# A graph network kernel: step tables of 32-bit words for the adjacency build, and its start moved to the 9th gather group

## The chip, the cores and the metric

The kernel runs on one core of a Trainium2 chip. The metric is the device time of one execution in microseconds (us), lower is better. An execution has four compute engines that run side by side: PE (TensorE, matmuls), DVE (VectorE), ACT (ScalarE) and POOL (GpSimd), and SP (SyncE), which issues transfers. Each has an instruction queue of its own, taken in order. They wait for each other on semaphores.

## The reference, cut to what matters

6,250 nodes of 128 features, 100,000 edges sorted by destination. Four graph layers in series, each added to its input. The third (`L2` in the reference) is itself three mean-aggregating layers over the same edges:

```python
def _sage_layer(x, src, dst, Wl, Wr, bias, n_nodes):
    msg_sum = jax.ops.segment_sum(x[src], dst, num_segments=n_nodes)
    cnt = jax.ops.segment_sum(jnp.ones((src.shape[0], 1), x.dtype), dst, num_segments=n_nodes)
    mean = msg_sum / jnp.maximum(cnt, 1.0)
    return mean @ Wl + x @ Wr + bias
...
h = jnp.maximum(_layernorm(x, axis=-1), 0.0)
x = x + _L0_gnn_ref(h, ...)
...
x = x + _L1_gnn_ref(h, ...)
...
x = x + _L2_gnn_ref(h, edge_index, L2_gnn_W_agg, L2_gnn_W_root, L2_gnn_b)
...
x = x + _L3_gnn_ref(h, ...)
```

## The kernel before, in words

The program walks eight internal layers, `k` = 0 to 7. The edges are cut into 784 tiles of 128, the tiles into 98 groups of 8. In the edge layers POOL gathers the source rows of each tile from DRAM by indirect DMA (L958), eight per group into one of two halves of `rows`. PE multiplies each tile by a one-hot matrix of its destinations (L1452), DVE adds the product into `acc` (L1925) and makes the one-hots two groups ahead (`make_onehot`, L1901). The gathers of a group wait until PE has multiplied the group two before.

Layer `k` = 2 does this and, beside it, **builds a dense adjacency matrix** in DRAM that layers 3 and 4 then multiply by (`dense_pass`) without gathering. The build is a chain of 1,567 steps. A step is one edge tile laid against one window of 8 destination nodes: 784 tiles and 784 windows in order are merged into one sequence. In step `i`:

- DVE (`mask_step`, L2068 and L2069) makes two masks: low digit of the source, and high digit of the source together with the place in the window. It may be up to 8 steps (`RING`) ahead of PE.
- PE (`adjacency_step`, L1430 to L1433) waits for the masks (`masked`) and for the evacuation two steps back (`evacuated`). It opens the next step's bank with a tiny matmul of zeros (L1431, 4 columns), then adds the outer product into this step's bank (L1432, 392 columns, bf16). There are four PSUM banks, 3 to 6.
- ACT (`evacuations`, L1097 to L1099) waits for that step (`stepped`) and for its own last evacuation (`evacuated`), and copies the bank's 49 x 8 words into a slab in `H`. SP writes a finished slab, 1,568 KB, to DRAM (`store_slabs`).

Which bank, which tile and which slab column belong to step `i` depends on the data, so the engines read them from tables in SBUF into registers. These loads stand in the engines' queues: PE loads 32 words of 16 bits every 16 steps (L1427), DVE 16 words of 16 bits every 16 steps (L2064), ACT 16 words of 16 bits and one more every 8 steps (L1108, L1111). The program is unrolled; register arithmetic (`FUSED_REGOPS` in the profile, `ISA` in the order of instructions) turns a register into an address behind the waits of its instruction.

The tables are made at the start of layer 2 (`plan`): DVE compares tile ends with step numbers (`compare_tiles`, L1989), PE sums the comparisons (`count_tiles`, L1412), DVE turns the sums into digits (`plan_steps`, L2008 to L2035). This takes four parts of up to 512 steps, and a fifth for the slabs (`plan_stores`). A part takes two groups, beginning at group `PLAN_FROM` = 2. The steps begin at group `STEP_FROM` = 14, 1,567 steps over 84 groups, which `steps_by` spreads evenly. In a group PE has its eight gather matmuls first and then its 18 or 19 steps. DVE runs `LEAD` = 6 masks ahead, then adds the eight products with masks in between. In groups 1 to 13 PE and DVE also have the dense products of the 13 chunks of nodes (`turn_rows`, `multiply_rows`, `take_product`), one chunk per group.

Of the kernel before, what the change touches and what calls it, by code (L numbers as in the profile page):

```python
# [15 lines left out]
P = 128  # L16
# [11 lines left out]
HT = 8  # L28
# [48 lines left out]
LOAD_REGS = 16  # L77
PLAN_FROM = 2
STEP_FROM = 14
# [9 lines left out]
def build(nc, a, out):  # L89
    ds = bass.ds  # L90
    with ExitStack() as ctx:
# [135 lines left out]
        def turned_at(k, c):  # L227

            at = 2048 if k in SAGE else 2560 + c % 2 * 512
            return PS[:, at:at + width(c)]  # L230

        def product_at(k, c):
            at = 2560 if k in SAGE else c % 2 * 512
            return PS[:, at:at + width(c)]

# [12 lines left out]
        def slack(k):  # L248
            return 0 if k in SAGE else 1
# [187 lines left out]
        counted_ps = PS[:, 6 * 512:7 * 512]  # L437
# [572 lines left out]
        def _(s):  # L1010
# [82 lines left out]
            evac_regs = [s.alloc_register(f"evac{j}") for j in range(2 * WN)]  # L1093

            def evacuate(i, first):
                s.wait_ge(stepped, i)
                s.wait_ge(evacuated, i)  # L1097
                to = H[:, ds(first[WN + i % WN], SLAB_WORDS)].rearrange("p (h d) -> p h d", d=SLABW)[:, :, 0:WN]
                nc.scalar.activation(to, PS[:, ds(first[i % WN], MASKW)].rearrange("p (h d) -> p h d", d=WN), ACT.Copy)\  # L1099
                    .then_inc(evacuated, 1)  # L1100

            def evacuations():
                s.wait_ge(tables_ready, 1)
                s.wait_ge(table_stored, 16 * table_parts[2])
                for i in range(STEPS + 1):
                    if i % WN == 0:
                        at = i // WN * 3 * WN
                        s.load(evac_regs, act_table[:, at:at + 2 * WN])  # L1108
                        first = [s.snap(r, min_val=3 * 512, max_val=6 * 512) for r in evac_regs[0:WN]]
                        first += [s.snap(r, min_val=0, max_val=SLAB_WORDS + SLABW - WN) for r in evac_regs[WN:2 * WN]]  # L1110
                        freed = s.value_load(act_table[:, at + 2 * WN:at + 2 * WN + 1], min_val=16, max_val=16 * SLABS)  # L1111
                        s.wait_ge(slabs_moved, freed)
                    if i > 0:
                        evacuate(i, first)
                    else:
                        s.wait_ge(edges_counted, PLANS + 2)
                        to = H[:, ds(first[WN], SLAB_WORDS)].rearrange("p (h d) -> p h d", d=SLABW)[:, :, 0:WN]
                        nc.scalar.activation(to, PS[:, ds(first[0], MASKW)].rearrange("p (h d) -> p h d", d=WN), ACT.Copy)\
                            .then_inc(evacuated, 1)
# [143 lines left out]
        def _(pe):  # L1263
# [158 lines left out]
            bank_regs = [pe.alloc_register(f"bank{j}") for j in range(2 * LOAD_REGS)]  # L1422
            bank_at = []

            def adjacency_step(i):
                if i % LOAD_REGS == 0:
                    pe.load(bank_regs, pe_table[:, 2 * i:2 * (i + LOAD_REGS)])  # L1427
                    bank_at[:] = [pe.snap(r, min_val=3 * 512, max_val=6 * 512 + MASKW) for r in bank_regs]
                wait(pe, evacuated, i - 1)
                pe.wait_ge(masked, i + 1)  # L1430
                mm(PS[:, ds(bank_at[LOAD_REGS + i % LOAD_REGS], 4)], ones_bf[:], zeros_bf[:, 0:4], start=True, stop=True)  # L1431
                mm(PS[:, ds(bank_at[i % LOAD_REGS], MASKW)], lo_slot(i), mask_slot(i), start=False, stop=True,  # L1432
# [1098 lines left out]
```

## Time and profile before

| | us |
|---|---|
| median of 3 runs | 11355.47 (11355.42 to 11371.14) |
| profiled execution | 11347.99 |
| its span | 11346.2 |

| engine | busy us | share of the span |
|---|---|---|
| PE | 5627.2 | 50% |
| DVE | 5247.5 | 46% |
| POOL | 4841.9 | 43% |
| ACT | 2131.4 | 19% |

The span is the time from the first to the last instruction of the profiled execution; its own device time is 1.8 us longer. No engine is busy for much over half of the span, so a share says little: each stage has its own limit, and has to be read apart. The granted clock of PE is given as a share of 2.4 GHz. Operations on registers and loads into them are not counted as busy; the idle time that they cause is shown as "issue".

### The profile page before, as it was taken

What the parts mean: (1) busy time and instruction counts of PE and PEld (TensorE: products, weight loads), DVE (VectorE), ACT (ScalarE), POOL (GpSimd) and SP (SyncE); (2) the same over time, 40 slices, a digit from 0 to 9 for tenths busy, and PEclk for the clock granted to TensorE, in tenths of its full rate; (3) what the DMA queues carried; (4) which work ended last, traced back from release to release, by engine and by line L of the source; (5) the groups of instructions that cost most, each with busy time, mean ns of one, the idle gap of its engine ahead of it and who ended that gap; (6) DMA issues with size and microseconds to landing.
All of it is one profiled execution on the core that took longest, in us unless ns stands there. A gap on an engine that the chain in (4) does not pass through costs nothing. (4 is left out here: it accounts for less than half of the span.)

```text
span 11346.2 us, 113568 instructions
## 1 busy us (share of the span) xinstructions
PE 5627.2 (50%) x27414; PEld 3519.3 (31%) x27414; DVE 5247.5 (46%) x17197; ACT 2131.4 (19%) x3703; POOL 4841.9 (43%) x5045
## 2 busy tenths in 40 slices
PE   5555555554444444445999804552306442216542
PEld 3333333323222222223444402352203442203432
DVE  6765566656333333443000105873308763219754
ACT  5555433331333333333000000000000000000000
POOL 5666466655222222221000173266570466650664
PEclk7766666666555555556999955566555665555756
DMA  5444456551222222223888721131230321220321
GB/s 163 136 133 140 141 162 172 162 146 49 81 80 81 81 74 81 85 82 111 297 284 291 238 79 36 52 98 41 56 95 6 93 72 36 75 72 19 101 59 34
DMA packets 728976, 1217.62 MB, mean 107 GB/s; under 512 B 109340, under 2 KB 547085, under 8 KB 714832
## 3 DMA queue, kind: packets, MB, share of 16 engines
q1 hardware_dynamic: 552716, 847.76, 22.2%
q0 software_dynamic: 161120, 311.32, 10.6%
q10 hardware_dynamic: 14688, 53.48, 1.2%
q8 instruction: 165, 2.70, 0.1%
q14 instruction: 287, 2.35, 0.1%
HBM read 865.31 MB, written 346.85 MB: 107 GB/s over the span
## 5 line engine op out<-in xcount | busy, mean ns | idle before, releaser
L988 POOL DMA_INDIRECT RO<-table,src_t x2346 | 2256.6, 962 | 3367.4 <-DMA table<-H 1287.9
L958 POOL DMA_INDIRECT RO<-table,src_t x2346 | 2242.8, 956 | 2919.5 <-PE PS L1452 1676.6
L1925 DVE TENSOR_TENSOR acc<-acc,PS 128x128 f32 x3910 | 1098.0, 281 | 1674.0 <-remote 1074.8
L1530 PE MATMUL PS<-RO 128*128 128x128 f32 x3060 | 649.1, 398 | 1136.7 <-DMA RO<-table,src_t 776.2
L1099 ACT ACTIVATE H<-PS x1567 | 779.4, 497 | 1716.3 <-issue 977.6
L1603 PE MATMUL PS<-als_bf,RO 128*128 128x49 bf16 x7056 | 397.4, 218 | 1192.5 <-issue 903.2
L1530 PEld LDWEIGHTS PS<-RO 128*128 128x128 f32 x3060 | 602.3, 301 | 1182.8 <-DMA RO<-table,src_t 797.3
L2363 DVE SCALAR_TENSOR_TENSOR H<-iota_row,srchi_t,PS 128x49 f32<-128x49 f32 x2352 | 461.1, 263 | 1086.2 <-remote 738.6
L1431 PE MATMUL PS<-work,ones_bf 3*128 3x4 bf16 x1567 | 279.3, 178 | 1356.4 <-issue 985.7
L2169 DVE TENSOR_SCALAR RO<-PS,loc_t,shared 128x128 f32<-128x128 f32 x2346 | 943.4, 404 | 0.6
L2068 DVE TENSOR_SCALAR bn<-work,shared 128x128 bf16<-128x128 int16 x1567 | 411.2, 262 | 1123.0 <-PE PS L1432 792.4
L1603 PEld LDWEIGHTS PS<-als_bf,RO 128*128 128x128 bf16 x7056 | 327.5, 118 | 1481.6 <-issue 1144.2
L1431 PEld LDWEIGHTS PS<-work,ones_bf 3*128 3x128 bf16 x1567 | 152.2, 97 | 1885.8 <-issue 1881.9
L1452 PE MATMUL PS<-RO 128*128 128x128 f32 x3128 | 593.5, 366 | 182.7 <-DMA RO<-table,src_t 97.2
L1452 PEld LDWEIGHTS PS<-RO 128*128 128x128 f32 x3128 | 579.9, 279 | 288.1 <-DMA RO<-table,src_t 132.0
L1530 PE MATMUL PS<-RO,H 128*128 128x128 f32 x1632 | 326.3, 382 | 264.6 <-issue 127.4
L1258 ACT ACTIVATE small<-small 128x49 f32<-128x49 f32 x3 | 0.7, 245 | 2283.9 <-issue 2283.9
L2351 DVE TENSOR_SCALAR RO<-PS,iota_col 128x1024 bf16<-128x1024 f32 x294 | 376.7, 1282 | 81.8 <-remote 52.4
L1490 PE MATMUL PS<-GT,H 128*128 128x512 f32 (+1 forms) x966 | 394.1, 565 | 1.4 <-DMA GT<-adjacency 1.4
L1530 PEld LDWEIGHTS PS<-RO,H 128*128 128x128 f32 x1632 | 304.6, 288 | 286.9 <-issue 286.9
L1490 PE MATMUL PS<-GT,acc 128*128 128x512 f32 (+1 forms) x952 | 392.3, 569 | 0.0
L1438 PE MATMUL PS<-shared,mats 128*128 128x512 f32 x392 | 323.4, 952 | 116.6 <-DVE shared L2121 67.7
(398 smaller groups left out, 8827.1 us busy)
## 6 DMA issues: line engine op xcount, KB each, us to landing
GT<-adjacency SPq DMA_DIRECT2D x126, 1792.0 KB, 7.2
adjacency<-H SPq DMA_DIRECT2D x98, 1568.0 KB
RO<-adjacency SPq DMA_DIRECT2D x42, 1792.0 KB, 7.2
RO<-table,src_t POOLq DMA_INDIRECT x4692
staged<-RO ACTq DMA_DIRECT2D x102, 512.0 KB
H<-staged SPq DMA_DIRECT2D x102, 512.0 KB
soft_rows<-shared SPq DMA_DIRECT2D x196, 256.0 KB
H<-soft_rows SPq DMA_DIRECT2D x98, 512.0 KB
```

The costliest lines, as they stand in the source:

```text
L958: pool.indirect_dma_start(rows[:, h * HT + j, :], None, table[k % 2], at(src_t[:, t:t + 1]))\
L988: pool.indirect_dma_start(rows[:, g % 2 * HT + j, :], None, table[k % 2], at(src_t[:, t:t + 1]))\
L1099: nc.scalar.activation(to, PS[:, ds(first[i % WN], MASKW)].rearrange("p (h d) -> p h d", d=WN), ACT.Copy)\
L1431: mm(PS[:, ds(bank_at[LOAD_REGS + i % LOAD_REGS], 4)], ones_bf[:], zeros_bf[:, 0:4], start=True, stop=True)
L1452: last = mm(window_at(k, c, j), rows[:, r, :], onehot[:, r, :], start=True, stop=True)
L1490: last = mm(sums_at(c).rearrange("p (s d) -> p s d", d=SLABW), of[:, t, :], slot_of(n)[:, 0:nslabs(c), j, :], start=(t == 0), stop=(t == N ...
L1530: last = mm(PS[:, o:o + D], block[:, j * D:(j + 1) * D], onehot[:, h * HT + j, :], start=True, stop=True)
L1603: last = mm(PS[:, o:o + NT], hot_bf[:, h, j, :], als_bf[:, part * NT:(part + 1) * NT], start=(part == 0), stop=(part == 2))
L1925: tt(at, at, window_at(k, c, j), ALU.add).then_inc(added[h], 1 if j < n - 1 else HT - n + 1)
L2068: ts(lo_slot(i), iota_16[:, 0:D], slo_t[:, ds(t, 1)], None, ALU.is_equal)
L2169: return ts(onehot[:, c % 2 * HT + j, :], iota_ps, loc_t[:, t:t + 1], ex_t[:, t:t + 1], ALU.is_equal, ALU.mult)
L2363: last = stt(mask[:, j, :], iota_row[:, 0:NT], srchi_t[:, ds(e, 1)], cand[:, j, :], ALU.is_equal, ALU.mult, accum_out=als_t[:, ds(e, 1)])
```

## The change

- `LOAD_REGS` falls from 16 to 8, and the tables are three rows of 32-bit words (`bank_row`, `column_row`, `tile_row`) and a small 16-bit one (`freed_row`), instead of 16-bit tables in which each engine's words stood together.
- PE loads 8 words every 8 steps. Both bank addresses are worked out in registers from one word. ACT loads 8 words every 8 steps and works its bank's address out from the slab column, by a division and a remainder. DVE loads 8 words every 8 steps.
- `plan_steps` has 14 operations instead of 20.
- A part of the plan takes one group instead of two, and DVE turns a part's sums into digits one group after they are counted. `STEP_FROM` is 8: 1,567 steps over 90 groups.
- The dense products take two chunks per group in layer 2, in banks 3 to 6. The plan's sums go to bank 7, which held a copy of `iota`; so the one-hots of layer 2 read `iota_row` in SBUF, and the copy in PSUM is made again in `plan_stores`.

```diff
@@
-LOAD_REGS = 16
+LOAD_REGS = 8
+BANKS = 4
+FIRST_BANK = 3
 PLAN_FROM = 2
-STEP_FROM = 14
+STEP_FROM = 8
@@ def turned_at(k, c) / product_at(k, c)
+            if k == 2:
+                at = 1536 + c % 2 * 512
...
+            if k == 2:
+                at = 2560 + c % 2 * 512
...
+        def chunks_beside(c):
+            return range(max(0, 2 * c), min(NCH, 2 * c + 2))
@@
-        pe_table = G[0:1, 1568:2 * 1568].bitcast(U16)
-        act_table = G[0:1, 2 * 1568:2 * 1568 + 2352].bitcast(U16)
-        dve_table = G[0:1, 2 * 1568 + 2352:2 * 1568 + 2352 + 784].bitcast(U16)
+        bank_row, column_row, tile_row = (G[0:1, (1 + i) * (STEPS + 1):(2 + i) * (STEPS + 1)].bitcast(I32)
+                                          for i in range(3))
+        freed_row = small[0:1, 4 * NT:6 * NT].bitcast(U16)
...
-        counted_ps = PS[:, 6 * 512:7 * 512]
+        counted_ps = PS[:, 7 * 512:8 * 512]
@@ def evacuations()
                 for i in range(STEPS + 1):
-                    if i % WN == 0:
...
-                        s.load(evac_regs, act_table[:, at:at + 2 * WN])
...
+                    if i % LOAD_REGS == 0:
+                        s.load(column_regs, column_row[:, i:i + LOAD_REGS])
+                        to = [s.snap(r, min_val=0, max_val=SLAB_WORDS + SLABW - WN) for r in column_regs]
+                        freed = s.value_load(freed_row[:, i // WN:i // WN + 1], min_val=16, max_val=16 * SLABS)
                         s.wait_ge(slabs_moved, freed)
...
+                    column = to[i % LOAD_REGS]
+                    bank_of = s.snap((column // WN) % BANKS * 512 + FIRST_BANK * 512, min_val=FIRST_BANK * 512,
+                                     max_val=(FIRST_BANK + BANKS - 1) * 512)
+                    wait(s, stepped, i)
+                    wait(s, evacuated, i)
@@ def adjacency_step(i)
                 if i % LOAD_REGS == 0:
-                    pe.load(bank_regs, pe_table[:, 2 * i:2 * (i + LOAD_REGS)])
...
+                    pe.load(bank_regs, bank_row[:, i:i + LOAD_REGS])
...
+                bank_now = bank_at[i % LOAD_REGS]
+                to = pe.snap(bank_now * 512 + FIRST_BANK * 512, min_val=FIRST_BANK * 512,
+                             max_val=(FIRST_BANK + BANKS - 1) * 512)
+                opened = pe.snap((bank_now + 1) % BANKS * 512 + FIRST_BANK * 512 + MASKW,
+                                 min_val=FIRST_BANK * 512 + MASKW, max_val=(FIRST_BANK + BANKS - 1) * 512 + MASKW)
@@ def edge_pass(k), PE
                     if k == 2:
-                        if c % 2 == 1 and 0 <= (c - PLAN_FROM) // 2 <= PLANS:
-                            count_tiles((c - PLAN_FROM) // 2)
+                        if 0 <= c - PLAN_FROM <= PLANS:
+                            count_tiles(c - PLAN_FROM)
@@ def make_onehot(k, c)
+                iota = iota_row[:] if k == 2 else iota_ps
@@ def plan(c), DVE
-                p, rest = divmod(c - PLAN_FROM, 2)
+                p = c - PLAN_FROM
+                if 0 < p <= PLANS:
+                    plan_steps(p - 1)
                 if 0 <= p <= PLANS:
-                    if rest == 0:
-                        compare_tiles(p)
...
+                    compare_tiles(p)
+                if p == PLANS + 1:
+                    plan_stores()
@@ def mask_step(i)
                 if i % LOAD_REGS == 0:
-                    v.load(tile_regs, dve_table[:, i:i + LOAD_REGS])
+                    v.load(tile_regs, tile_row[:, i:i + LOAD_REGS])
```

How the instructions stand before and after, at three places. `ISA` rows are register arithmetic, and `[waits ...]` names the semaphores that a row waits for.

PE in the build, around a register load; before:

```order
L1432 ISA
L1432 MATMUL PS<-cut_row,bn 128x392
L1427 TENSOR_LOAD GT
L1428 ISA x4
L1431 ISA [waits masked,evacuated]
L1431 MATMUL PS<-work,ones_bf 128x4
L1432 ISA
L1432 MATMUL PS<-shared,bn 128x392
```

and after:

```order
L1442 ISA
L1442 MATMUL PS<-cut_row,bn 128x392
L1432 TENSOR_LOAD GT
L1433 ISA
L1441 ISA [waits masked,evacuated]
L1441 MATMUL PS<-work,ones_bf 128x4
L1442 ISA
L1442 MATMUL PS<-shared,bn 128x392
```

The load stands in the same place, 8 words instead of 32, and comes every 8 steps. The `ISA` ahead of the small matmul holds two operations on registers before and six after (an addition, a remainder by 4, two multiplications, two additions); the one ahead of the large matmul two before and four after.

ACT in the build, around a register load; before:

```order
L1099 ACTIVATE H<-PS 128x49x8
L1108 TENSOR_LOAD GT
L1109 ISA
L1110 ISA
L1111 TENSOR_LOAD GT
L1111 ISA x2
L1099 ISA [waits evacuated,stepped,slabs_moved]
L1099 ACTIVATE H<-PS 128x49x8
```

and after:

```order
L1122 ACTIVATE H<-PS 128x49x8
L1113 TENSOR_LOAD GT
L1114 ISA
L1115 TENSOR_LOAD small
L1115 ISA x2
L1122 ISA [waits evacuated,stepped,slabs_moved]
L1122 ISA
L1122 ACTIVATE H<-PS 128x49x8
```

Two `ISA` now stand between the waits and the copy: six operations (a division by 8, a remainder by 4, two multiplications, two additions) and two, where one `ISA` of four stood.

PE ahead of the build, between the gather matmuls of two groups; before:

```order
L1452 MATMUL PS<-RO 128x128 [waits added1]
L1452 MATMUL PS<-RO 128x128 x3
L1318 MATMUL PS<-mats,mid 128x128 [waits p_done,p_copied]
L1318 MATMUL PS<-mats,mid 128x128 x3
L1305 MATMUL PS<-ident,H 128x128 [waits p_copied,h_chunks]
L1305 MATMUL PS<-ident,H 128x128 x3
L1452 MATMUL PS<-RO 128x128 [waits added1,onehot_ready1,gathered1]
```

and after:

```order
L1323 MATMUL PS<-mats,mid 128x128 [waits p_done,p_copied]
L1323 MATMUL PS<-mats,mid 128x128 x3
L1323 MATMUL PS<-mats,mid 128x128 [waits p_done,p_copied]
L1323 MATMUL PS<-mats,mid 128x128 x3
L1310 MATMUL PS<-ident,H 128x128 [waits p_copied,h_chunks]
L1310 MATMUL PS<-ident,H 128x128 x3
L1310 MATMUL PS<-ident,H 128x128 [waits p_copied,h_chunks]
L1310 MATMUL PS<-ident,H 128x128 x3
L1417 MATMUL PS<-cut_row,small 128x512 [waits tiles_compared]
L1417 MATMUL PS<-cut_row,small 128x512 x3
L1417 MATMUL PS<-bn,small 128x512 x3
L1462 MATMUL PS<-RO 128x128 [waits added0,onehot_ready0,gathered0]
```

Each of these groups now has two chunks of dense products, and a count that waits for DVE's comparisons of the same group (`tiles_compared`), ahead of the next group's gather matmuls.

## Rows read from the trace of the kernel before

**Rows 1.** windows of the layer-2 pass: lead-in, build. Columns as in the first line.
```profile
core 0: us, PE busy (x) PEld busy (x) DVE busy (x) ACT busy (x) POOL busy (x), PEclk, DMA share, GB/s
2647.40:2831.00 183.60, 86.15 (x424) 73.94 (x424) 114.87 (x297) 7.45 (x13) 123.70 (x128) 0.65 0.17 46
2831.00:5330.00 2499.00, 1142.88 (x4458) 583.80 (x4458) 1000.61 (x3874) 779.91 (x1569) 620.77 (x654) 0.56 0.22 80
```

**Rows 2.** waits in the build (2831 to 5330 us): us in total, times, longest.
```profile
PE PS L1431 <- issue: 985.7, 127, 11.3
ACT H L1099 <- issue: 977.6, 392, 7.5
```

**Rows 3.** register loads, each from the view of its line: duration ns min/median/max.
```profile
L1427 PEldq TENSOR_LOAD <-GT x98: 7516/10073/10575, 2822.4 to 5305.9; - x98
...
L1108 ACTq TENSOR_LOAD <-GT x196: 3367/3392/6607, 2809.0 to 5319.4; - x196
...
L2064 DVEq TENSOR_LOAD <-GT x98: 3582/3594/4121, 2817.9 to 5297.1; - x98
...
L1057 ACTq TENSOR_LOAD <-rank_row x65: 289/310/917, 1190.2 to 11292.4; - x65
...
L1910 DVEq TENSOR_LOAD <-seg_row x490: 593/597/1756, 61.4 to 11266.2; - x164
```

**Rows 4.** timeline of ACT in the build: start, length, in brackets idle before.
```profile
3519.38 0.50 ACT L1099 ACTIVATE H<-PS  x1 [4.03 <-issue]
3520.07 0.50 ACT L1099 ACTIVATE H<-PS  x1 [0.19 <-ACT H L1099]
...
3526.56 0.50 ACT L1099 ACTIVATE H<-PS  x1 [2.58 <-PE PS L1432]
```

**Rows 5.** timeline of PE in the same stretch.
```profile
3522.61 3.44 PE L1452 MATMUL PS<-RO 128*128 128x128 f32 x16
...
3535.15 0.18 PE L1431 MATMUL PS<-work,ones_bf 3*128 3x4 bf16 x1 [8.35 <-ACT H L1099]
```

**Rows 6.** ACT's register arithmetic and one-register load, by line: ns min/median/max.
```profile
L1099 ACTq FUSED_REGOPS  x1567: 6/55/508, 2834.2 to 5329.2; - x196
...
L1110 ACTq FUSED_REGOPS  x196: 126/126/131, 2812.6 to 5323.6; - x196
...
L1111 ACTq TENSOR_LOAD <-GT x196: 263/269/273, 2812.8 to 5323.8; - x196
L1111 ACTq FUSED_REGOPS  x196: 167/168/191, 2813.1 to 5324.1; - x196
```

**Rows 7.** timeline of DVE in the same stretch.
```profile
3514.10 1.22 DVE L1901 TENSOR_TENSOR RO<-PS,loc_t 128x1024 f32<-128x1024 f32 x1
...
3519.27 0.25 DVE L2068 TENSOR_SCALAR bn<-work,shared 128x128 bf16<-128x128 int16 x1 [3.05 <-issue]
...
3519.73 0.25 DVE L2068 TENSOR_SCALAR bn<-work,shared 128x128 bf16<-128x128 int16 x1
...
3526.18 0.29 DVE L1925 TENSOR_TENSOR acc<-acc,PS 128x128 f32 x1 [4.16 <-PE PS L1452]
```

**Rows 8.** timeline of DVE ahead of the build.
```profile
2703.81 3.22 DVE L1925 TENSOR_TENSOR acc<-acc,PS 128x128 f32 x8 [6.12 <-remote]
...
2708.68 0.68 DVE L2009 SCALAR_TENSOR_TENSOR GT<-work,PS 128x512 f32<-128x512 int16 x1
...
2718.65 0.43 DVE L2035 TENSOR_SCALAR GT<-GT 128x512 f32<-128x512 f32 x1
...
2725.03 1.13 DVE L1989 TENSOR_SCALAR cut_row<-work,small 112x512 bf16<-112x512 int16 x4
```

**Rows 9.** timeline of PE: a count of the plan, and the build's first step.
```profile
2727.95 1.91 PE L1412 MATMUL PS<-cut_row,small 112*128 112x512 bf16 x4
2729.65 1.20 PE L1412 MATMUL PS<-bn,small 112*128 112x512 bf16 x3
...
2831.11 0.18 PE L1431 MATMUL PS<-work,ones_bf 3*128 3x4 bf16 x1 [4.75 <-issue]
```

More of the change, by code:

```diff
@@ L1091, in normalize @@
                     normalized_rows(k, c - 1)
[L1093 to L1100, printed above, removed]
+            column_regs = [s.alloc_register(f"column{j}") for j in range(LOAD_REGS)]
             def evacuations():
@@ L1420, in open_banks @@
                     .then_inc(edges_counted, 1)
-            bank_regs = [pe.alloc_register(f"bank{j}") for j in range(2 * LOAD_REGS)]
+            bank_regs = [pe.alloc_register(f"bank{j}") for j in range(LOAD_REGS)]
             bank_at = []
@@ L1453, in edge_pass @@
                     last.then_inc(multiplied[h], 1)
-                    if 1 <= c <= NCH:
+                    if k == 2:
+                        for m in chunks_beside(c - 1):
+                            multiply_rows(k, m)
+                        for m in chunks_beside(c):
+                            turn_rows(k, m)
+                    elif 1 <= c <= NCH:
                         multiply_rows(k, c - 1)
-                    if c < NCH:
+                    if k == 0 and c < NCH:
                         turn_rows(k, c)
@@ L2006, in plan_steps @@
                 n = plan_width(p)
+                part = slice(p * PW, p * PW + n)
                 v.wait_ge(edges_counted, p + 1)
-                w = window_cols[:, p * PW:p * PW + n]
+                w = window_cols[:, part]
                 step(stt(w, iota_16[:, 0:n], float(p * PW), counted_ps[:, 0:n], ALU.add, ALU.subtract))
-                step(copy(dve_table[:, p * PW:p * PW + n], counted_ps[0:1, 0:n]))
+                step(copy(tile_row[:, part], counted_ps[0:1, 0:n]))
                 row, a, b = w[0:1, :], int_a[0:1, 0:n], int_b[0:1, 0:n]
-                in_loads = b.rearrange("o (g w) -> o g w", w=LOAD_REGS)
@@ L2013, in plan_steps @@
-                in_eights = b.rearrange("o (g w) -> o g w", w=WN)
-                def digits_of(shift, mask):
-                    step(ts(a, row, float(shift), None, ALU.add))
-                    step(ts(b, a, mask, None, ALU.bitwise_and))
-                digits_of(0, 3)
-                step(ts(by_load(pe_table, p, 0), in_loads, 512.0, 3.0 * 512, ALU.mult, ALU.add))
-                digits_of(1, 3)
-                step(ts(by_load(pe_table, p, 1), in_loads, 512.0, 3.0 * 512 + MASKW, ALU.mult, ALU.add))
@@ L2023, in plan_steps @@
-                digits_of(3, 3)
-                step(ts(by_evacuations(p, 0), in_eights, 512.0, 3.0 * 512, ALU.mult, ALU.add))
-                digits_of(15, 15)
+                step(copy(a, row))
+                step(ts(bank_row[:, part], a, BANKS - 1, None, ALU.bitwise_and))
+                step(ts(a, row, 15.0, None, ALU.add))
+                step(ts(b, a, 15, None, ALU.bitwise_and))
                 step(ts(a, b, 3, None, ALU.arith_shift_right))
                 step(ts(a, a, float(SLAB_WORDS - SLABW), None, ALU.mult))
-                step(stt(by_evacuations(p, 1), in_eights, float(WN), a.rearrange("o (g w) -> o g w", w=WN),
-                         ALU.mult, ALU.add))
+                step(stt(column_row[:, part], b, float(WN), a, ALU.mult, ALU.add))
@@ L2092, in gather_and_build @@
                     if c + 2 < NG:
-                        make_onehot(c + 2)
-                    if 1 <= c <= NCH:
-                        take_product(2, c - 1)
+                        make_onehot(2, c + 2)
+                    for m in chunks_beside(c - 1):
+                        take_product(2, m)
                     plan(c)
@@ L2481, in _ @@
                     step(memset(acc[:], 0.0), zeros_ready)
-                if k == 2:
-                    step(copy(iota_ps, iota_row[:]))
                 if k in DENSE:
```

55 lines of the change are left out of this document (20 added, 35 removed).

## The prediction, made before the changed kernel ran

> **What bounds the kernel now.** I read the windows first. Layer 2 starts gathering at 2647, the build's first step on PE is at 2831.1 and the build ends at 5330: 2,499 us, 22% of the span, in which PE is busy 1,143 us, DVE 1,001, ACT 780, POOL 621 and the DMA engines 22% [rows 1, 9]. No engine is full, so something that is not counted as busy sets the pace. The waits name it: PE and ACT each stood 980 us at "issue", waiting for nothing but their own queue, and PE's 127 such waits reach 11.3 us [rows 2].
>
> The views of the single lines show what the queues did. PE's load of 32 words takes 10.07 us and comes 98 times: 98 x 10.07 = 987 us. ACT's load of 16 words takes 3.39 us and comes 196 times, DVE's of 16 words 3.59 us [rows 3]. The two timelines show the effect. Ordinarily one evacuation follows the other by 0.50 + 0.19 = 0.69 us (3519.38 to 3520.07). At a load of ACT the gap is 4.03 us, at a load of PE 8.35 us; and while PE does the 16 passes of a group's gather matmuls, 3.44 us, ACT drains the two steps in hand and then stands 2.58 us [rows 4, 5]. As a check I add these for the whole build: 987 for PE's loads; 98 x 3.84 = 376 for those of ACT's loads that don't fall beside one of PE's (4.03 - 0.19 = 3.84); 1,568 evacuations x 0.685 = 1,074; 84 groups x 2.4 = 202. That is 2,639, 6% over the 2,499 measured, since some loads begin under gather matmuls. So the model is good to some 6%, on the high side.
>
> **The loads.** The three loads of the build read 16-bit words, at 0.315 us a word on PE, 0.21 to 0.22 on ACT and DVE. But the kernel also has loads of 32-bit words: ACT's of four takes 0.310 us and DVE's of eight 0.597 us, both 0.075 to 0.078 us a word [rows 3]. The changed kernel makes exactly DVE's form, eight 32-bit words, on three engines. I take 0.60 us for each; for PE, whose 16-bit words cost 1.4 times DVE's, 0.84. The upper end for a word is the 16-bit price: 1.7 us on ACT and 2.5 on PE for eight. A lower end is four words' 0.31.
>
> The Trainium skill ("Runtime: NRT & Kernel Launch", Instruction fetch mechanics) states that a TENSOR_LOAD costs about 200 ns a register, even in bulk. By that, eight words would be 1.6 us. The trace agrees for 16-bit words (212 ns) and speaks against it for 32-bit ones (75 ns).
>
> **ACT's step.** The new register arithmetic stands behind both waits of an evacuation, so it lengthens every step of the chain. Before, one `ISA` of four operations takes 0.055 us [rows 6]. After come one of six, with a division and a remainder that the trace shows nowhere, and one of two. Bounds: six plain operations of another kind take 0.126 us (L1110), 0.021 each; three comparisons take 0.168, 0.056 each [rows 6]. At the cheap rate the eight cost some 0.17 us, at the dear one 0.45. I take plain operations at 0.014 (0.055 / 4) and the two unknown ones at the dear 0.056, plus 0.03 to start a second `ISA`: 6 x 0.014 + 0.112 + 0.03 = 0.22, 0.165 more than now. A step becomes 0.685 + 0.165 = **0.85 us**; bounds 0.77 and 1.08.
>
> **ACT's load boundary.** Now 3.84 us over an ordinary gap. It loses 3.39 - 0.60 = 2.79, and L1110 with its start and two operations, 0.19; the one-word load (0.26) and its checks (0.17) stay. 0.86 is left; 0.9 with something for loads of two engines at once, which slow each other (L1108 reaches 6.6 us) [rows 3, 6].
>
> **PE's load boundary.** 0.84 plus one `ISA` of eight, about 0.17: 1.0 us every 8 steps. It runs beside ACT's boundary of 0.9 at the same steps. PE may be two evacuations ahead: from an evacuation's end to the evacuation three further on there are three ACT steps, 2.55 us, and the work in between is some 0.4 us of register work and signals, 0.1 and 0.5 of matmuls and 0.7 on ACT, 1.7 us. The 0.85 us of slack covers the load but for 0.2, which ACT's own boundary covers. So 0; without that cover, 196 x 1.0.
>
> **DVE.** A pair of masks takes 0.46 us (3519.27 to 3519.73), a one-hot of eight tiles 1.2; each group DVE waits 4.2 us for PE's gather matmuls [rows 7]. A group has 17.4 steps: 17.4 x 0.46 = 8.0, eight adds at 0.2 in between 1.6, one-hot 1.2, loads of tiles 2.2 x 0.7 = 1.5, load of segments 1.0, together 13.3, and 17.5 with the wait. That is under the 18.9 us of a group found below, so it is hidden by 1.4 us a group, no more. The one-hot from SBUF instead of PSUM moves as many elements and is taken at the same 1.2.
>
> **Gather matmuls.** Now 2.4 us of ACT's time a group. Two slower evacuations cover 0.33 more; PE's new register work in the restart and mixed clocks leave 2.1 us, in 90 groups. POOL's indirect DMAs, busy 621 us in the build before [rows 1], take 684 for 90 groups, 40% of the new build. A slab comes every 17 us or so; DMA engines at 22% go to about 33%. Neither counts.
>
> **The lead-in.** Up to group 3's adds (2703.8) it is as before. DVE turned a part into digits in 2708.68 to 2719.08, 10.4 us for 20 operations; 14 take about 7.2. Four comparisons take 1.1 us, so seven 2.0 [rows 8]. Groups 3 to 5 each have adds 3.2, one-hot 1.1, two products 1.3, digits 7, comparisons 2 = 14.7. Then PE's count of this group (three of seven matmuls 1.2 us, so about 3 [rows 9]) and the next gather's 3 to 4 come in series, because the count waits for the comparisons: 22 us. Groups 6 and 7 are smaller (a part of 32 steps, then slabs), 15 and 11. 2704 + 3 + 66 + 15 + 11 = 2799, with the first load 2800, against 2831 [rows 9]: **-31 us**, give or take 15.
>
> **The sum.** Build: 1,568 x 0.85 = 1,333, plus 196 x 0.9 = 176, plus 90 x 2.1 = 189: **1,698 us**, against 2,499. Gain 801 + 31 = 832. A group is 1,698 / 90 = 18.9. The profiled execution took 11,348; less 832 is **10,516 us**. It lies 7 us under the median, less than I can resolve. With the bounds of ACT's step alone: 0.77 gives 10,391, 1.08 gives 10,877.
>
> **Rivals.**
> - *DVE takes over.* If the new register operations are as cheap as the old ones (step 0.77), ACT's chain gives 1,573 us and DVE's 17.5 us x 90 = 1,575. Then the time stops at 1,575: 10,393. For it: additions and multiplications cost 14 ns; against: a division is no addition. 0.13.
> - *PE's clock rises.* It was 0.56 in the build, so mostly 1.2 GHz [rows 1], with PE busy 46%; in the new build the same work fills 70%. At 2.4 GHz the gather matmuls halve, and most of 90 x 1.7 = 153 us goes: 10,365. 0.07.
> - *Loads cost by the register, whatever the type.* ACT's eight words at 0.212 are 1.7 us, 1.1 more than taken, x 196 = 216; PE's 2.5 run beside them, but exceed ACT's boundary by half a microsecond: up to 98 more. 10,730 to 10,830. Against it stand two rows of 32-bit loads [rows 3]; for it, that neither is on PE. 0.07. The 200 ns a register of the Trainium skill ("Runtime: NRT & Kernel Launch", Instruction fetch mechanics) would come to the same.
> - *Register division and remainder are dear, though not ruinous*: 0.15 us each instead of 0.056 add 0.19 x 1,568 = 295: 10,810. 0.09.
> - *They cost more than the loads did* (slower). Both stand behind ACT's waits in each of 1,568 steps, and nothing hides them. The gain of 832 is gone at 832 / 1,568 = 0.53 us a step more than taken, so from 0.32 us for each of the two. At 0.4 each the step is 1.54 and the time 10,516 + 0.69 x 1,568 = 11,600. Against it: no register operation in the rows is over 0.056 us. 0.04, of which 0.01 falls within 0.2% of no change.
>
> **How the numbers follow.** My forecast, 10,430 to 10,620, has 0.60. The range must reach DVE's and the clock's case below and part of the dearer ones above: 10,350 to 10,760. Outside lie some 0.05 below and 0.13 above. A difference of 0.2% is about what a measurement of this kernel tells from none. Faster by more than that: every case but the last, 0.96; within it 0.01; slower 0.03.
>
> **What the profile after will show.** Right: TENSOR_LOAD of eight at 0.6 us on ACT and DVE and under 0.9 on PE; register arithmetic of ACT near 0.22 in its two `ISA`; evacuations 0.85 apart, with gaps of 1.2 us every eight; "issue" waits on PE nearly gone; first step at 2800, last near 4500. Wrong: an eight-word load over 1.5 us; ACT's step over 1 us; DVE with no wait for the gather matmuls, or PE waiting for masks in most steps, which makes DVE the bound; a granted clock far over 0.56 in the build; or time that moves into layers 3 and 4.

## The result, and the profile after

The changed kernel takes 10,660.19 us (median of 4 runs, 10,642.40 to 10,671.95) against 11,359.05 us of the kernel before (4 runs, 11,355.42 to 11,371.14): a ratio of 0.9384, 95% interval 0.9373 to 0.9396. The profiled execution took 10,670.19 us, its span is 10,668.4. The forecast was 10,516 with a range of 10,350 to 10,760: the time lies inside, but above the inner 10,430 to 10,620 that I gave 0.60, and of a forecast gain of 832 us only 699 came. Identical programs ran in two kinds of execution here, in which the kernel before takes 11,348 to 11,413 us or 9,600 to 9,612 us; I call them long and short, all of the runs named so far are long ones, and each experiment is read against runs of its own kind.

The windows of the changed kernel, lead-in and build, answer to [rows 1]; the columns are the same.

```profile
core 0: us, PE busy (x) PEld busy (x) DVE busy (x) ACT busy (x) POOL busy (x), PEclk, DMA share, GB/s
2647.40:2803.00 155.60, 60.87 (x334) 51.84 (x334) 92.16 (x252) 15.21 (x37) 77.74 (x78) 0.65 0.15 40
2803.00:4645.60 1842.60, 1182.35 (x4552) 609.83 (x4551) 1042.60 (x3935) 779.33 (x1568) 708.23 (x704) 0.59 0.31 111
```

The build is 1,843 us instead of 2,499, with the same 780 us of evacuations in it. PE's share rises from 46% to 64%, the granted clock only from 0.56 to 0.59: still mostly the lower of its two levels.

The views of the single lines, in order PE's, ACT's and DVE's load, ACT's word on the freed slab, and the register arithmetic of PE's two matmuls and of ACT's evacuation (ns min/median/max), answer to [rows 3, 6]:

```profile
L1432 PEldq TENSOR_LOAD <-GT x196: 587/591/1432, 2800.6 to 4637.1; - x196
...
L1113 ACTq TENSOR_LOAD <-GT x196: 4/547/1711, 2801.2 to 4638.0; - x196
...
L2060 DVEq TENSOR_LOAD <-GT x196: 5/597/2045, 2800.5 to 4630.7; - x196
...
L1115 ACTq TENSOR_LOAD <-small x196: 5/267/885, 2802.0 to 4638.7; - x196
L1115 ACTq FUSED_REGOPS  x196: 14/168/710, 2802.3 to 4639.0; - x196
...
L1441 PEldq FUSED_REGOPS  x1567: 104/104/131, 2802.1 to 4643.5; - x196
...
L1442 PEldq FUSED_REGOPS  x1567: 60/60/70, 2802.3 to 4643.7; - x196
...
L1122 ACTq FUSED_REGOPS  x3136: 4/37/716, 2802.5 to 4645.4; - x196
```

Eight 32-bit words take 0.55 to 0.60 us on all three engines, so PE's loads fell from 987 us in the build to 196 x 0.59 = 116. The last row mixes two instructions of each evacuation, one of six operations at 0.143 or 0.147 us and one of two at 0.037 (when taken apart). Its longest is 0.716 us, where ACT's arithmetic before had a longest of 0.508 [rows 6]. That is the mark of what I had not foreseen.

The waits in the build answer to [rows 2] (us in total, times, longest):

```profile
ACT H L1122 <- PE PS L1442: 625.2, 755, 3.6
ACT H L1122 <- issue: 269.4, 326, 18.9
...
PE PS L1441 <- ACT H L1122: 349.8, 727, 2.9
PE PS L1441 <- issue: 166.1, 256, 3.2
PE PS L1441 <- DVE cut_row L2065: 89.4, 97, 2.2
PE PS L1441 <- DVE shared L2065: 51.7, 90, 2.2
...
DVE acc L1941 <- PE PS L1462: 401.9, 89, 5.3
DVE bn L2064 <- PE PS L1442: 286.8, 423, 2.9
...
POOL RO L970 <- PE PS L1462: 896.6, 87, 15.7
```

PE's "issue" waits have gone from 986 us to 166. Now ACT and PE wait for one another: the ring of steps is the bound. DVE still waits for PE, as it would not if it set the pace.

The timeline of ACT shows an ordinary stretch and then the unforeseen one (columns as in [rows 4]):

```profile
3614.15 0.50 ACT L1122 ACTIVATE H<-PS  x1 [0.34 <-ACT H L1122]
3614.98 0.50 ACT L1122 ACTIVATE H<-PS  x1 [0.34 <-issue]
3615.82 0.50 ACT L1122 ACTIVATE H<-PS  x1 [0.34 <-ACT H L1122]
3616.66 0.50 ACT L1122 ACTIVATE H<-PS  x1 [0.34 <-issue]
3618.92 0.50 ACT L1122 ACTIVATE H<-PS  x1 [1.77 <-issue]
3620.54 0.50 ACT L1122 ACTIVATE H<-PS  x1 [1.12 <-issue]
3621.83 0.50 ACT L1122 ACTIVATE H<-PS  x1 [0.80 <-ACT H L1122]
3622.67 0.50 ACT L1122 ACTIVATE H<-PS  x1 [0.34 <-PE PS L1442]
```

Evacuations start 0.84 us apart. From 3616.66 to 3621.83 three take 5.17 us. One load of ACT's falls in it, so 3.35 would be ordinary; PE does no gather matmul. What stands between them are ACT's short queue instructions (a wait on a semaphore, a register operation): some take 0.70 us here instead of 0.02 to 0.15, and others begin only 0.7 us after the one before. I counted those that take 0.5 us or more in the trace, loads left out: 270 on ACT in the build, 150 on DVE, none on PE, in some 90 stretches of about 4 us, one to each gather group, 6 to 12 us after the start of its first gather on POOL. In the kernel before they were 5 on ACT, 51 on DVE and 4 on PE.

I then took the distance of every two evacuations, and what it exceeds 0.837 us by, or 1.67 at a load. The build of 1,843 us is

| part of the build | us | forecast |
|---|---|---|
| 1,568 steps x 0.837 | 1,312 | 1,333 |
| 196 load boundaries x 0.83 | 163 | 176 |
| excess while PE does a group's gather matmuls, 89 groups x 1.59 | 141 | 189 |
| excess where ACT's short instructions take 0.7 us | 207 | none |
| the rest | 19 | none |

### The profile page after: what moved, and what is told of

It is laid out like the page before. It is cut to its first block and busy times, and to the rows that moved or that the text cites. A ratio compares the mean times of both kernels' runs of the same rounds, so it can differ in the third digit from the quotient of the medians.

```text
span 10668.4 us, 114911 instructions
## 1 busy us (share of the span) xinstructions
PE 5650.2 (53%) x27414; PEld 3518.0 (33%) x27414; DVE 5257.7 (49%) x17169; ACT 2130.5 (20%) x3703; POOL 4883.4 (46%) x5045
## 5 line engine op out<-in xcount | busy, mean ns | idle before, releaser
L1618 PE MATMUL PS<-als_bf,RO 128*128 128x49 bf16 x7056 | 396.9, 218 | 1182.7 <-issue 857.4
L1618 PEld LDWEIGHTS PS<-als_bf,RO 128*128 128x128 bf16 x7056 | 327.4, 118 | 1472.2 <-issue 1075.9
```

Source lines behind the costliest of these rows:

```text
L1618: last = mm(PS[:, o:o + NT], hot_bf[:, h, j, :], als_bf[:, part * NT:(part + 1) * NT], start=(part == 0), stop=(part == 2))
```

## The experiments

**First four runs: which part gives what, and what makes the slow stretches.** The kernel before took 11,413.27 us beside them, a long execution, 54 us over the first. The changed kernel itself did not run beside these four, and each was run once, so differences below some 100 us in them are weak.

*e1_words16*: the tables hold 16-bit words again, still eight to a load (and the plan has one more copy on DVE, not shown).

```diff
-        bank_row, column_row, tile_row = (G[0:1, (1 + i) * (STEPS + 1):(2 + i) * (STEPS + 1)].bitcast(I32)
+        bank_row, column_row, tile_row = (G[0:1, (1 + i) * (STEPS + 1):(1 + i) * (STEPS + 1) + (STEPS + 1) // 2].bitcast(U16)
```

> The changed kernel with its three tables as 16-bit words again, still eight to a load every eight steps. Theory (a word's type sets the price): ACT's load of eight goes from 0.55 to about 1.7 us, PE's from 0.59 to about 2.4, DVE's to 1.8; ACT's load boundary grows by some 1.15 us, so the build by 196 x 1.15 = 225 us, and the time goes to about 10,890. Rival (what costs is more than eight registers in one load, or a load as such): the loads stay near 0.6 us and the time near 10,665.

Measured: 10,892.86 us, build 2,046 us. The loads of ACT, PE and DVE in this kernel:

```profile
L1113 ACTq TENSOR_LOAD <-GT x196: 8/1728/4729, 2803.4 to 4843.5; - x196
...
L1432 PEldq TENSOR_LOAD <-GT x196: 1923/1927/3884, 2802.9 to 4842.7; - x196
...
L2061 DVEq TENSOR_LOAD <-GT x196: 13/1832/4932, 2802.9 to 4835.2; - x196
```

Eight words of 16 bits cost 1.73, 1.93 and 1.83 us, the same eight as 32-bit words 0.55, 0.59 and 0.60. Of the loads only the type differs, so the type sets the price: 0.22 to 0.24 us a word against 0.07. The build grew by 203 us; 196 x (1.73 - 0.55) = 231. Taken apart as above, the load boundaries cost 230 us more, but the stretches of slow short instructions only 120 us instead of 207, and other gaps 58 more. So the time agrees with the expected 10,890 in part by luck; the loads' price does not rest on it. PE's share of the 16-bit price was less than the 0.315 us a word of [rows 3]: with eight words instead of 32 it was 0.24.

*e2_start14*: one line, `STEP_FROM = 14` instead of 8.

> The changed kernel with the steps beginning at group 14 again; all else as changed. Theory (the earlier start is a small part): first step near 2,860 instead of 2,803, six groups fewer beside the build, so the build some 35 us shorter, time about 10,685 (+20). Rival (the earlier start carries the gain): the time goes back by hundreds of us.

Measured: 10,814.32 us, first step 2,882.1 (79 us later), build 1,893 us, 50 longer than the changed kernel's. That is far over the expected 10,685, by more than the 54 us of the kernel before beside it. I had not expected a longer build; the last experiment repeats this kernel.

*e3_few_rows*: the gathers beside the build fetch 8 rows of 128. What the left-out 120 rows would give is missing from layer 2's sums.

```diff
+                        n = 8 if k == 2 and g >= STEP_FROM else P
-                        pool.indirect_dma_start(rows[:, h * HT + j, :], None, table[k % 2], at(src_t[:, t:t + 1]))\
+                        pool.indirect_dma_start(rows[0:n, h * HT + j, :], None, table[k % 2], at(src_t[0:n, t:t + 1]))\
```

> Gathers beside the build fetch 8 of their 128 rows (so layer 2's sums and all after are other numbers); as many instructions and signals as before. In the trace of the changed kernel ACT's queue has one stretch a group, 6 to 12 us after the group's gathers began, in which short instructions take 0.7 us each; 2.3 us of delay a group. Theory G (the gathers' transfers cause it): the stretches vanish, the build falls from 1,842 to about 1,640 us and the time to about 10,460. Rivals (instruction supply, slab stores, VectorE's one-hot): they stay and the time is 10,650 +- 25.

Measured: 10,808.84 us, build 1,959 us, and 274 slow short instructions on ACT, 207 on DVE: no fewer than with all rows. The volume of the gathers does not make the stretches. The time is over both of my cases; by the count above the stretches cost some 315 us here.

*e4_onehot_psum*: DVE reads the row of numbers for its one-hots from PSUM during the build, as before.

```diff
-                iota = iota_row[:] if k == 2 else iota_ps
+                iota = iota_row[:] if k == 2 and c < STEP_FROM + 2 else iota_ps
```

> In the build the one-hots read iota from PSUM again instead of SBUF. Theory P (two SBUF operands of VectorE beside POOL's work cause the slow stretches in the queues): they vanish, time about 10,460. Rival (they come from elsewhere): no change, 10,650 +- 25, one-hot 1.22 us in both.

Measured: 10,781.17 us, build 1,917 us, 297 and 179 slow short instructions, some 275 us of stretches. The reading place does not make them either, and again the time is over both cases. In the changed kernel a one-hot took 1.218 us from SBUF and 1.217 from PSUM, as forecast.

**Next four: the terms of the step, and the changed kernel once more.** Here the kernel before took 9,608.24 us (7 runs, 9,600.16 to 9,612.34): short executions, though on the chip of the first four.

*e5_changed_again*: no edit.

> The changed kernel unaltered, on the chip of the next three: 10,660 on its first chip, 10,670 to 10,730 here if the chip adds what the last one added to before (54 us). Adjacency build 1,843 us, 0.837 us from one evacuation to the next, one slow stretch of ACT's and DVE's queues to each gather group (270 short instructions of 0.7 us on ACT, 150 on DVE).

Measured: 8,717.94 us, ratio 0.9074 (0.9058 to 0.9089), nowhere near the 10,670 to 10,730 expected. So the change gains 890 us here, and 699 in the long executions. The build is 1,643 us, with no slow short instruction on DVE and no slow register operation on ACT.

```profile
core 0: us, PE busy (x) PEld busy (x) DVE busy (x) ACT busy (x) POOL busy (x), PEclk, DMA share, GB/s
2386.80:4030.20 1643.40, 1192.67 (x4553) 616.01 (x4552) 1026.59 (x3936) 779.35 (x1567) 714.62 (x705) 0.60 0.35 124
```

PE, ACT, DVE and POOL are busy for the same time as in the long execution within 2%, and the clock is the same. The 199 us between the two builds are idle time, against the 207 us counted for the slow stretches. By the same count the gather matmuls cost 152 us here, 1.7 a group.

*e6_ahead_of_waits*: ACT forms the bank address into a register ahead of the two waits of a step, and in a shorter form, without the division.

```diff
-                    bank_of = s.snap((column // WN) % BANKS * 512 + FIRST_BANK * 512, min_val=FIRST_BANK * 512,
-                                     max_val=(FIRST_BANK + BANKS - 1) * 512)
+                    s.reg_mod(bank_reg, column, WN * BANKS)
+                    s.reg_mul(bank_reg, bank_reg, 512 // WN)
+                    s.reg_add(bank_reg, bank_reg, FIRST_BANK * 512)
+                    hold(s)
+                    bank_of = s.snap(bank_reg, min_val=0, max_val=8 * 512 - MASKW)
```

> ACT's bank address is formed into a register ahead of the two waits of a step (modulo, product and sum, 0.15 us), instead of behind them. Theory A (an evacuation's period is ACT's and PE's round trip, and the 0.147 us of arithmetic behind the wait lies on it): 0.837 becomes 0.69 to 0.71 us, the build 1,843 less 1568 x 0.14 = 1,620, the time 10,440 to 10,480. Rival B (PE's own step, or the evacuation itself, sets the period): 0.80 or more stays, the build 1,790 or more. If the slow stretches come from the number of instructions that ACT takes in, this kernel, which has one or more further queue instructions per step, shows more than 270 slow ones on ACT; if they go with the gather group's start, the number stays about 90 stretches.

Measured: 8,562.80 us, ratio 0.8914 (0.8899 to 0.8929), 155 us under e5. The instruction behind the waits is short again,

```profile
L1126 ACTq FUSED_REGOPS  x1567: 60/60/65, 2385.2 to 3869.6; - x196
```

and the step is 0.689 us, the 0.15 less that theory A says. Rival B falls. What stands behind the waits went from 0.184 us in two instructions to 0.060 in one. The new form is also cheaper, 0.077 us ahead of the waits (a remainder 0.040, product and sum 0.037) where it had 0.147 behind them; I estimate from these durations that some 0.05 of the 0.15 is the shorter form's and the rest the move's. No run separates the two. Of 1,568 x 0.15 = 235 us the build gave 158 (1,485 us): the gather matmuls now cost some 190 us instead of 152, which I put down to ACT's draining sooner what PE has in store; the distance at a load stayed, 1.70 us where it was 1.67, which costs 34; and 7 went to other gaps.

*e7_split_gather*: four steps between the two halves of a group's gather matmuls.

```diff
+                        if j == 4:
+                            for i in range(steps_by(c - 1), steps_by(c - 1) + split):
+                                adjacency_step(i)
...
-                        for i in range(steps_by(c - 1), steps_by(c)):
+                        for i in range(steps_by(c - 1) + split, steps_by(c)):
```

> A group's eight gather matmuls are given in two halves with four adjacency steps between them, so that PE is away from the steps for about 1.7 us at a time instead of 3.4. Theory A (each group's gather matmuls cost the chain of steps 1.57 us because they are longer than the one step that the ring of four banks holds in store): the excess at gathers falls from 141 to under 60 us, the build to 1,760, the time to 80 less than the changed kernel. Rival: every return of PE costs its own start, two halves cost as much as one whole, and the time stays within 20.

Measured: 8,614.67 us, ratio 0.8965 (0.8950 to 0.8980), 103 us under e5; build 1,537 us, 106 less, and the excess at gathers 47 us instead of 152. The stall at the gather matmuls is what PE's absence exceeds the store by; two short absences cost little.

*e8_all_three*: both edits, with masks 10 steps ahead (`LEAD = 10`) and the word on the freed slab read at the middle of eight steps.

```diff
+                        if i == 0:
+                            freed = s.value_load(freed_row[:, 0:1], min_val=16, max_val=16 * SLABS)
                         s.wait_ge(slabs_moved, freed)
+                    if i % LOAD_REGS == LOAD_REGS // 2 and i + LOAD_REGS // 2 < STEPS + 1:
+                        n = i // WN + 1
+                        freed = s.value_load(freed_row[:, n:n + 1], min_val=16, max_val=16 * SLABS)
```

> Both edits, the word on the freed slab read at the middle of eight steps instead of between the load and the first evacuation, and masks 10 steps ahead of PE instead of 6. If nothing else takes over: 1568 x 0.70 + 196 x 0.55 + 91 x (0.6 + 2.3) = 1,470 us of build. DVE's groups need 17.5 us each, 91 x 17.5 = 1,590, so DVE is likely to take over: build 1,590 to 1,640, time 10,410 to 10,470, 200 to 250 under the changed kernel on this chip.

Measured: 8,452.85 us, ratio 0.8797 (0.8782 to 0.8812): 265 us under the changed kernel and 1,155 under the one before, in short executions. The edits of e6 and e7 alone gave 155 and 103, 258 together, so the further masks and the moved word show no clear gain of their own; the word costs at its new place too (the distance there is 1.48 us in the median, where 0.689 is ordinary).

```profile
core 0: us, PE busy (x) PEld busy (x) DVE busy (x) ACT busy (x) POOL busy (x), PEclk, DMA share, GB/s
2405.90:3781.20 1375.30, 1142.08 (x4551) 601.20 (x4551) 1004.22 (x3935) 778.80 (x1568) 736.78 (x704) 0.62 0.41 148
```

The build is 1,375 us. My 1,590, at which DVE was to take over, was wrong: of the 17.5 us a group that I gave DVE, 4.2 were its wait for PE's gather matmuls, which shrinks when they are split (154 us over 87 waits here, 1.8 each). A group now takes 1,375 / 90 = 15.3 us, PE is busy 83% of it.

**Next three: both kernels in one kind of execution.** Short again (before: 9,604.38 us), on another chip.

*e9_before_again* and *e10_changed_again*: no edits, for a trace of each.

> The kernel before, unaltered, for its trace. The last job's executions of before and of the changed kernel were 1,750 and 1,940 us shorter than the first ones of the same programs, and the changed kernel's build (1,643 instead of 1,843 us) held no slow stretch of ACT's and DVE's queues. If such an undisturbed execution is met again (about 9,608 us): first step at 2,410 to 2,440 us, build 2,440 to 2,500 us, no slow short instruction on DVE where the first trace had 51, and so before's build hardly shorter than the 2,499 us of the first trace. If the disturbance costs both kernels the same in the build, as a mere slowing of everything would, before's build comes out 200 us shorter, at 2,300.

> The changed kernel unaltered beside the last one, once more for its trace. Undisturbed: 8,718 us, build 1,643 us, no slow stretch. Disturbed: 10,660 to 10,730 us, build 1,843 to 1,900 us, 270 slow short instructions on ACT and 150 on DVE. Whichever it is, the run of before beside it is of the same kind.

Measured: 9,607.32 and 8,716.99 us. The kernel before, windows and the lines of ACT's arithmetic and PE's and ACT's loads:

```profile
core 0: us, PE busy (x) PEld busy (x) DVE busy (x) ACT busy (x) POOL busy (x), PEclk, DMA share, GB/s
2428.80:4925.20 2496.40, 1147.63 (x4455) 588.09 (x4454) 994.12 (x3868) 778.42 (x1567) 618.58 (x654) 0.56 0.22 80
...
L1099 ACTq FUSED_REGOPS  x1567: 55/55/70, 2428.6 to 4925.0; - x196
...
L1427 PEldq TENSOR_LOAD <-GT x98: 7517/10074/10583, 2419.3 to 4901.8; - x98
...
L1108 ACTq TENSOR_LOAD <-GT x196: 3367/3394/6589, 2403.9 to 4915.3; - x196
```

and ACT's evacuation and load in the changed kernel:

```profile
L1122 ACTq FUSED_REGOPS  x3136: 37/96/182, 2392.3 to 4036.0; - x196
...
L1113 ACTq TENSOR_LOAD <-GT x196: 537/547/1707, 2390.9 to 4028.5; - x196
```

The extremes differ from those of the long executions: ACT's arithmetic took 6 to 508 ns before [rows 6] and 55 to 70 here, in the changed kernel 4 to 716 ns and 37 to 182 here. The medians of single forms in the build are the same. Set side by side, long less short execution, from first and last evacuation of each trace:

| | kernel before | changed kernel |
|---|---|---|
| ahead of the build | 406 | 410 |
| the build | 2,495.0 - 2,496.4 = -1 | 1,842.7 - 1,643.5 = 199 |
| behind the build | 1,337 | 1,344 |
| whole span | 1,741 | 1,953 |

What lengthens an execution costs both kernels the same, within 8 us, everywhere but in the build. There the kernel before pays nothing, and the changed kernel 199 us. Most of what is paid behind the build is paid by PE's queue: the matmuls of `candidates` (L1618), in loops of later layers, stand in three blocks of 2,352, beside gathers of POOL. A block takes 262 us in the short execution and 631 to 665 in the long one, where for 350 us and more a matmul starts only every 3 us or so. The long execution's waits of PE have this row, and the short one's have none at "issue" for the line:

```profile
PE PS L1618 <- issue: 857.4, 321, 17.7
```

In the kernel before the blocks take 262 us against 641 to 667. Between the build and the first block, in layers 3 and 4, POOL is busy for 23 us of 1,140, and there the same instructions of the kernel before stay 403 to 404 us apart in the two executions: nothing is slowed there. In short executions the gain is 853 us in the build and 36 ahead of it, 890 in all. The rival that everything slows alike (before's build at 2,300) falls. The build without slow stretches has the length that was expected (2,440 to 2,500).

*e11_more_words*: four further register instructions in ACT's queue for each evacuation, ahead of the waits.

```diff
-                    column = to[i % LOAD_REGS]
+                    r = column_regs[i % LOAD_REGS]
+                    for by in (1, -1, 2, -2, 3, -3):
+                        s.reg_add(r, r, by)
+                        hold(s)
+                    column = s.snap(r, min_val=0, max_val=SLAB_WORDS + SLABW - WN)
```

> The changed kernel, with four further register instructions in ACT's queue per evacuation (the column plus and minus small numbers), ahead of the waits, where ACT has time. Theory R (the slow stretches come when ACT and DVE take in more instructions than arrive): the number of slow short instructions rises well above that of the changed kernel beside it (from 270 to 500 or more where the execution is disturbed; above 50 where it isn't), and the build grows by 100 us or more. Rival O (an outside condition that comes with the gathers' start and doesn't heed how many instructions an engine takes): about 90 stretches of the same 4 us stay, with more short instructions hit in each at most in proportion, and undisturbed there are none; the build stays within 40 us beyond what the further instructions themselves take from the period.

Measured: 8,734.92 us, build 1,651 us instead of 1,643.5, no slow short instruction in it. ACT's queue took 6,271 further instructions (4,704 and 1,567 of 0.029 us) at a cost of 8 us. So the number of instructions does not bring the stretches by itself. Whether it brings more of them in a long execution, where theory R could still hold, was not to be seen in this short one.

**Last run.** *e12_start14_again*: the kernel of e2 once more. It met a long execution (before: 11,353.28 us).

> The steps begin behind group 14 again and all else stays as changed (the second run's kernel). Undisturbed, and beside 8,717 us of the changed kernel: first step 77 to 80 us later than 2,393 (as before, 2,882.1 - 2,802.9), five or six groups' gather stalls less in the build (6 x 1.6 = 10 us, so 1,634 instead of 1,643 us), time 8,780 to 8,790. Rival, after the second run, whose build was 50 us longer than the changed kernel's: a late start lengthens the build itself, to 1,690, and the time is 8,840. If the execution is disturbed, the time tells nothing new and only the first step counts.

Measured: 10,722.20 us, first step 2,858.7, build 1,844 us, 245 slow short instructions on ACT in 81 stretches. I had said that in a long execution only the first step would count. It is 56 us later than the changed kernel's, and that is what the early start is shown to give. The time is 62 us over the changed kernel's, with a kernel before within 6 us, and the build is the same, so the whole fits: some 60 of the 699 us. The rival from e2 (a late start lengthens the build) falls; e2's 50 us were for the most part slow stretches (247 us by the same count, 208 here), whose cost differs between executions. e1, e3 and e4 have to be read with that spread in mind: what they show is the loads' price and that the stretches stay, not differences of 50 us.

## Why the prediction was right, and where its sum was off

- **What bounds it** was right: register loads in the queues. PE's "issue" waits fell from 986 to 166 us, and in e1 the words' type alone puts 230 us back into the load boundaries.
- **The loads**, 0.60 us on ACT and DVE and 0.84 on PE: measured 0.55, 0.60 and 0.59. PE's surcharge of 1.4 was needless. The rival of loads priced by the register has fallen for 32-bit words. The Trainium skill ("Runtime: NRT & Kernel Launch", Instruction fetch mechanics) gives about 200 ns a register even in bulk; the runs come near it for 16-bit words (216 to 241 ns in e1) and not for 32-bit ones (68 to 75 ns). The page speaks of registers loaded from HBM, though, and the tables here lie in SBUF, which the prediction passed over; so the runs limit its figure and do not refute it.
- **ACT's step**, 0.85 us from 0.055 + 0.165: measured 0.837, with arithmetic of 0.147 and 0.037. Division and remainder are hardly dearer than the rest: six operations with both take 0.147, six others 0.126 [rows 6]. Both rivals on them have fallen. The 0.03 us taken for the start of a second `ISA` had no row behind it; the step grew by 0.152 and the arithmetic by 0.129, which leaves 0.02. e6 shows that the arithmetic lay on the chain in full: 0.124 us less of it behind the waits, and one `ISA` less, made each step 0.15 shorter.
- **ACT's load boundary**, 0.9: measured 0.83. **PE's load boundary**, 0: e8 takes ACT's one-word load out of the boundary and leaves PE's in it, and the distance of the two evacuations there falls from 1.70 us (e6) to 1.16, so PE's load had not held it above that. No run took PE's load away alone.
- **The lead-in**, -31 us: the first evacuation went from 2,834.3 to 2,802.9, 31.4 earlier. The size is right, but in part by luck: that the start alone is worth 56 (e12) means that other parts of the change cost the lead-in some 25 us, and I did not find which.
- **The gather matmuls**, 2.1 us a group in 90 groups: measured 1.6 and 1.7. The mechanism was right (e7 takes 106 us out), the term 37 to 48 us too large.
- **DVE** was hidden, as said. But its 17.5 us a group held a wait of 4.2 that is PE's doing; as a limit for later changes the figure was wrong (e8).
- **The clock** stayed at 0.58 to 0.62 of full speed in the builds of both kinds, short of the rise that would have halved the gather matmuls. That rival fell.
- **The missing term** is the step that failed: the sum 1,333 + 176 + 189 has none for time in which ACT's queue itself is slow. It was 207 us in the first profile. In a short execution, where it is absent, the build took 1,643 us against the forecast of 1,698. In the first profile the three terms came to 1,616 us instead of 1,698, and 207 + 19 us had no term: 226 - 82 = 144 in the build. The profiled execution missed by 10,670 - 10,516 = 154, so the build holds nearly all of the miss; that the median's miss, 10,660 - 10,516, is 144 too is chance. It was luck that three terms were 82 us too large: exact ones would have put the forecast at some 10,434 and the miss at 226.

The trace of the kernel before had marks of it that I passed over: a longest of 0.508 us and a shortest of 6 ns for an instruction whose median is 0.055 [rows 6], and 51 short instructions of 0.5 us and more on DVE in the build. They cost the kernel before nothing (2,495.0 us of build against 2,496.4); that its queues stood in loads of 3.4 and 10 us anyway would explain it, but is not shown. And they could not tell how many there would be.

**What stays open.** What slows the queues is not found. Shown is: it comes and goes between executions of one program (the kernel before, on one chip: long beside e1 to e4, short beside e5 to e8); in the build it follows the start of a gather group by 6 to 12 us, hits ACT and DVE and hardly PE, while later in the program it is PE's queue that stands; and it depends neither on the rows that the gathers move (e3) nor on the place of DVE's operand (e4). The slab stores do not set it off: in the first profile 85 of 93 stretches begin 5.6 to 9.5 us after the start of a gather group, half of them within 7.1 to 7.9, but anywhere from 1 to 16 us after the last store was issued. Slower fetching of instructions does not show in their transfers: in the build there are 186 packets of them in the long execution of the changed kernel and in the short one, and over the whole span those of the busier queue take 0.42 us each in the mean in both. That the stretches need a certain rate of instructions is a guess that would explain why before's build had hardly any on ACT, and why e1, with longer loads, had 120 us of them instead of 207; e11 could not test it. Leaving out all gathers, or their issue on POOL, was not tried. e6 to e8 were not seen in a long execution, so their gains hold for short ones.

## What to carry to other kernels

Read a register table as 32-bit words, and price a load by the type: eight words cost a third of what eight 16-bit words cost. When a long stall goes, the path left is made of queue instructions of 20 to 150 ns; put those that need no signal ahead of the waits and keep them short (e6: 155 us for both), and read minimum and maximum of such instructions, not their median alone (6 and 508 ns against 55 and 70 here), for here they told the two kinds of execution apart. Split a block of other work on PE in two where a ring of buffers covers half of it but not the whole (e7: 103 us).

## What the runs showed that I had not expected

- One program has two kinds of execution here, 9,608 and 11,359 us for the kernel before, with equal instruction counts and, in the build, equal medians of single instructions and an equal clock. Whole-time ratios differ between them (0.9074 and 0.9384), so a change must be compared within one kind.
- In the long kind, short instructions of ACT's and DVE's queues take 0.70 us in the build, in stretches of some 4 us tied to the gather groups: 199 us for the changed kernel's build, nothing for the one before. Behind the build PE's queue is the slow one, a matmul every 3 us or so for 350 us and more beside POOL's gathers, three times.
- A 16-bit word costs 0.22 to 0.24 us to load, eight at a time, on ACT, DVE and PE; a 32-bit word 0.07.
- Six register operations in one instruction, with a division and a remainder, take 0.147 us; two more in a second one 0.037.
